# A transformer layer on 8 cores: the transposed `fc` weights are kept in DRAM, loads are merged, and two weight loads move ahead of their fences

## What is computed

```python
def _L0_attn_ref(x, W_q, W_kv, W_o):                 # H = 16 heads of 128
    q  = (x @ W_q.T).reshape(B, S, H, hd)
    kv = (x @ W_kv.T).reshape(B, S, H, hd)
    qf, kvf = fft(q), fft(kv)                        # over the head's 128
    qf, kvf = qf / |qf|, kvf / |kvf|                 # norm over the last axis
    kvf = cumsum(kvf, axis=1)                        # over the tokens
    values = ifft(qf * kvf).real.reshape(B, S, D)
    return values @ W_o.T

def _L0_ffn_ref(x, W_fc, W_proj):                    # 2048 -> 8192 -> 2048
    h  = square(relu(x @ ternary(W_fc).T))
    hn = h * rsqrt(mean(h * h) + eps)
    return hn @ ternary(W_proj).T

x = x + layernorm(_L0_attn_ref(layernorm(x), W_q, W_kv, W_o))
x = x + layernorm(_L0_ffn_ref(layernorm(x), W_fc, W_proj))
```

## Time and profile before

| | |
|---|---|
| time, 2 runs | 5866.28 and 5962.6 us, median 5914.44 |
| the profiled execution | 5843.32 us; span 5841.6 us on the slowest core (core 1) |
| cores' spans | 5798.1 to 5841.6 us |
| granted TensorE clock, mean | 0.77 on every core |
| stage 4 (feed-forward) | 3469 to 5841 us, 2372 us |

### The profile page before, as it was taken

One profiled execution on the slowest core, in us unless ns is written; L12 is line 12 of the kernel. 1 busy time (PEld: TensorE's weight loads), 2 busy tenths in 40 slices (PEclk: granted clock), 3 DMA queues, 4 the chain that ended last, 5 costly groups with the idle time before them and its releaser, 6 DMA issues.

```text
span 5841.6 us, 42698 instructions; the slowest of 8 cores (5798.1 to 5841.6 us)
## 1 busy us (share of the span) xinstructions
PE 3024.2 (52%) x12580; PEld 1194.8 (20%) x12580; DVE 2177.9 (37%) x2629; ACT 956.5 (16%) x1081; POOL 239.0 (4%) x420
## 2 busy tenths in 40 slices
PE   0404041404024024141455549994999589958995
PEld 0101010101001001010111114441334233423342
DVE  5465656561795791524122222103210221022202
ACT  2232323230232230101000011101110111001100
POOL 0000000000010010101000000000000000000000
PEclk9756565757557557575777789997999799979997
DMA  6353534354343435464742227544854375438542
GB/s 177 97 147 105 144 108 150 102 138 92 115 144 100 117 132 131 124 135 123 164 90 58 58 62 132 107 143 114 133 106 143 115 130 108 144 112 139 104 144 99
DMA packets 895779, 699.47 MB, mean 120 GB/s; under 512 B 694466, under 2 KB 768578, under 8 KB 879170
## 3 DMA queue, kind: packets, MB, share of 16 engines
q1 hardware_dynamic: 746178, 386.17, 28.7%
q0 software_dynamic: 68096, 201.35, 11.4%
q10 hardware_dynamic: 81280, 109.21, 7.7%
HBM read 411.24 MB, written 159.51 MB: 98 GB/s over the span
## 4 chain that ended last, share of the span: by engine, by line
PE 46%; DMA 20%; DVE 16%; issue 9%; another core or an unknown queue 4%; ACT 3%; SPq 2%; ACTq 0%; DVEq 0%; POOLq 0%; POOL 0%
PE pall L817 16%; PE pall L863 15%; PE pall L365 5%; DMA arena<-pj_t 5%; PE pall L710 4%; DVE arena L459 4%; DVE arena L441 4%; DMA pjT_t<-arena 3%; DMA arena<-b_scr 2%; SPq L802 2%; DMA fc_t<-arena 2%; DMA arena<-rq_scr 2%; DMA arena<-qn_scr 1%; PE pall L793 1%
## 5 line engine op out<-in xcount | busy, mean ns | idle before, releaser
L817 PE MATMUL pall<-arena 128*128 128x512 bf16 x4096 | 935.8, 382 | 43.9 <-DMA arena<-fc_t 32.8
L863 PE MATMUL pall<-arena 128*128 128x512 bf16 x4096 | 900.8, 383 | 30.7 <-DVE arena L871 27.0
L365 PE MATMUL pall<-arena 128*128 128x512 bf16 x2048 | 486.6, 393 | 651.8 <-DMA arena<-x_scr 216.0
L280 PE MATMUL pall<-arena,tones 128*1 128x512 bf16 x192 | 88.4, 469 | 853.7 <-DMA arena<-xT 632.4
L863 PEld LDWEIGHTS pall<-arena 128*128 128x128 bf16 x4096 | 403.8, 99 | 526.9 <-issue 54.4
L817 PEld LDWEIGHTS pall<-arena 128*128 128x128 bf16 x4096 | 382.5, 98 | 533.0 <-issue 112.9
L435 ACT ACTIVATE arena<-arena 128x2048 bf16<-128x2048 f32 x128 | 244.3, 1908 | 874.5 <-DMA pj_t<-arena 424.6
L827 DVE TENSOR_TENSOR arena<-arena 128x512 bf16<-128x512 bf16 x256 | 108.9, 425 | 743.5 <-ACT arena L824 743.5
L871 DVE TENSOR_TENSOR arena<-pall,rows 128x512 bf16<-128x512 f32 x64 | 44.3, 692 | 909.8 <-PE pall L863 903.7
L365 PEld LDWEIGHTS pall<-arena 128*128 128x128 bf16 x2048 | 195.8, 100 | 915.6 <-issue 716.7
L617 PE MATMUL pall<-arena,tdft 128*128 128x512 bf16 x64 | 37.6, 587 | 587.0 <-DMA arena<-qn_scr 587.0
(11 more groups left out here) (93 smaller groups left out, 2165.4 us busy)
## 6 DMA issues: line engine op xcount, KB each, us to landing
arena<-wfc SPq DMA_DIRECT2D x64, 1024.0 KB, 5.5
arena<-wproj SPq DMA_DIRECT2D x64, 1024.0 KB, 5.8
arena<-pjT_t SPq DMA_DIRECT2D x256, 256.0 KB, 2.7
arena<-pjT_t ACTq DMA_DIRECT2D x256, 256.0 KB, 2.7
fc_t<-arena POOLq DMA_DIRECT2D x64, 512.0 KB, 3.4
pj_t<-arena POOLq DMA_DIRECT2D x64, 512.0 KB, 4.5
pjT_t<-arena POOLq DMA_DIRECT2D x64, 512.0 KB, 3.0
arena<-xT POOLq DMA_DIRECT2D x8, 2048.0 KB, 15.7
```

The source lines that it names most:

```text
L365: last = h.matmul(pbks[i % 2], w3[:, k, m * P:(m + 1) * P], c2(src, k), start=(k == 0), stop=(k == NK - 1))
L817: last = h.matmul(bk(bi), pieces[pi][:, k * 1024 + m8 * P:k * 1024 + (m8 + 1) * P], c2(x3_bf, k), start=(k == 0), stop=(k == NK - 1))
L863: last = h.matmul(bk(j8), stripe[si][:, j8 * P:(j8 + 1) * P], c2(h2, m), start=(m == 0), stop=(m == NMH - 1))
```

## The change

1. 64 background steps are added between those of `pj_t` and `pjT`: `fcT_thunk(k, q4)` transposes a [2048, 128] piece of `fc_t` through `pt_buf` into the new DRAM tensor `fcT_t` [2048, 8192]. There are 256 steps now for the 298 places.
2. Stage 4's first pass loads an eighth with one plain DMA of 4 MB (128 x 16 rows of 2 KB) from `fcT_t`: on SP for the even eighths, on ACT for the odd ones.
3. The second pass loads two stripes with one DMA of 512 KB, into one of two buffers, in turn on SP and ACT.
4. The loads of `wkvT` and `woT` are recorded ahead of the fence instead of behind it. They go to the same SBUF space and wait for the last reader of the weights before.

```diff
+            def fcT_thunk(k, q4):
+                def thunk():
+                    em.dma("sync", lambda h: h.dma_start(
+                        out=pt_buf[0][:, :],
+                        in_=fc_t[q4 * D:(q4 + 1) * D, k * P:(k + 1) * P],
+                        transpose=True),
+                        reads=tuple(f"fct_{t}" for t in range(NMH)),
+                        writes=("ptb",))
+                    em.dma("gpsimd", lambda h: h.dma_start(
+                        out=fcT_t[k * P:(k + 1) * P, q4 * D:(q4 + 1) * D],
+                        in_=pt_buf[0][:, :]),
+                        reads=("ptb",), writes=(f"fcTt{k}",))
+                return thunk
+
+            for k in range(NK):
+                for q4 in range(HID // D):
+                    pwork.append(fcT_thunk(k, q4))
...
+        for kq in range(4 if PHASES >= 3 else 0):
+            em.dma("gpsimd", lambda h, kq=kq: h.dma_start(
+                out=wq_sb.rearrange("p (k m) -> p k m", m=D)[:, 4 * kq:4 * kq + 4, :],
+                in_=wkvT.rearrange("(k p) m -> p k m", p=P)[:, 4 * kq:4 * kq + 4, :]),
+                reads=(f"wq{kq}",), writes=(f"wq{kq}", f"wkv{kq}"))
+
         em.fence()
...
-        stripe = [ar.bf16(1024) for _ in range(4)]
+        stripe = [ar.bf16(2048) for _ in range(2)]
...
             for oct_ in range(8):
                 pi = oct_ % 2
-                for k in range(NK):
-                    em.dma("sync" if (k % 2 == 0 or not OPT & 4) else "scalar",
-                           lambda h, pi=pi, k=k, oct_=oct_: h.dma_start(
-                        out=pieces[pi][:, k * 1024:(k + 1) * 1024],
-                        in_=fc_t[oct_ * 1024:(oct_ + 1) * 1024,
-                                 k * P:(k + 1) * P], transpose=True),
-                        reads=FCT, writes=(f"pc{pi}_{k}",))
-                pks = tuple(f"pc{pi}_{k}" for k in range(NK))
+                em.dma("sync" if oct_ % 2 == 0 else "scalar",
+                       lambda h, pi=pi, oct_=oct_: h.dma_start(
+                    out=pieces[pi][:, :].rearrange("p (k e) -> p k e", e=1024),
+                    in_=fcT_t.rearrange("(k p) e -> p k e", p=P)
+                    [:, :, oct_ * 1024:(oct_ + 1) * 1024]),
+                    reads=FCTT, writes=(f"pc{pi}_0",))
+                pks = (f"pc{pi}_0",)
...
-                for m in range(NMH):
-                    si = m % 4
-                    em.dma("sync" if (m % 2 == 0 or not OPT & 2) else "scalar",
-                           lambda h, si=si, m=m, jo=jo: h.dma_start(
-                        out=stripe[si][:, :],
-                        in_=pjT_t[m * P:(m + 1) * P,
-                                  jo * 1024:(jo + 1) * 1024]),
-                        reads=PJT, writes=(f"st{si}",))
...
+                for mp in range(NMH // 2):
+                    sp = mp % 2
+                    em.dma("sync" if mp % 2 == 0 else "scalar",
+                           lambda h, sp=sp, mp=mp, jo=jo: h.dma_start(
+                        out=stripe[sp][:, :].rearrange(
+                            "p (mm e) -> p mm e", e=1024),
+                        in_=pjT_t.rearrange("(mm p) e -> p mm e", p=P)
+                        [:, 2 * mp:2 * mp + 2,
+                         jo * 1024:(jo + 1) * 1024]),
+                        reads=PJT, writes=(f"st{sp}",))
```

More of the change, by code:

```diff
@@ L197, in build_nc @@
     pjT_t = nc.dram_tensor("pjT_t", [HID, D], BF16, kind=_ikind).ap()
+    fcT_t = nc.dram_tensor("fcT_t", [D, HID], BF16, kind="Internal").ap()
     x1_scr = nc.dram_tensor("x1_scr", [D, SEQ], BF16, kind=_ikind).ap()
@@ L569, in build_nc @@
         B_t = [ar.bf16(T) for _ in range(2)]
-        for kq in range(4 if PHASES >= 3 else 0):
-            em.dma("gpsimd", lambda h, kq=kq: h.dma_start(
-                out=wkv_sb.rearrange("p (k m) -> p k m", m=D)[:, 4 * kq:4 * kq + 4, :],
-                in_=wkvT.rearrange("(k p) m -> p k m", p=P)[:, 4 * kq:4 * kq + 4, :]),
-                writes=(f"wkv{kq}",))
         WKVK = tuple(f"wkv{i}" for i in range(4))
@@ L661, in build_nc @@
             drain(8)
+        for kq in range(4 if PHASES >= 4 else 0):
+            em.dma("gpsimd", lambda h, kq=kq: h.dma_start(
+                out=wkv_sb.rearrange("p (k m) -> p k m", m=D)[:, 4 * kq:4 * kq + 4, :],
+                in_=woT.rearrange("(k p) m -> p k m", p=P)[:, 4 * kq:4 * kq + 4, :]),
+                reads=(f"wkv{kq}",), writes=(f"wkv{kq}", f"wo{kq}"))
         em.fence()
@@ L673, in build_nc @@
         bc23 = ar.bf16(2 * T)
-        for kq in range(4 if PHASES >= 4 else 0):
-            em.dma("gpsimd", lambda h, kq=kq: h.dma_start(
-                out=wo_sb.rearrange("p (k m) -> p k m", m=D)[:, 4 * kq:4 * kq + 4, :],
-                in_=woT.rearrange("(k p) m -> p k m", p=P)[:, 4 * kq:4 * kq + 4, :]),
-                writes=(f"wo{kq}",))
         WOK = tuple(f"wo{i}" for i in range(4))
@@ L772, in build_nc @@
         r_rms = rows[0:1, 3 * T + T // 2:3 * T + T].bitcast(BF16)
-        FCT = tuple(f"fct_{t}" for t in range(NMH))
+        FCTT = tuple(f"fcTt{t}" for t in range(NK))
         PJT = tuple(f"pjTt{m}" for m in range(NMH))
```

23 lines of the change are left out of this document (14 added, 9 removed).

## The result

The changed kernel takes 6734.38 us, the median of 11 runs; the kernel before, on the same chips, takes 5984.08, the median of 10. The ratio of their comparable runs is 1.141, with an interval from 1.132 to 1.150. The forecast was 6600, so the time came out 134 us above it: inside the range of 6410 to 6800, and above the 6520 to 6690 that the forecast had for itself. In a part of the executions of every kernel the cores of one die, or of both, show a lower granted clock and are some per cent slower; they are in the medians, whose difference of 750 us is therefore no measure of the change, and not in the ratios, and where an experiment met mostly such executions, its lowest run, or the cores without it, are compared. What the change adds is seen in the two profiled executions: 6667.64 - 5843.32 = 824 us, and 14.1% of the lowest 5866 is 825 too. The sum had +729, so it was 95 us short.

What follows compares the result with a forecast made beforehand. It took TensorE to bound stage 4 (feed-forward), with the transposing loads hidden. The sum 5843.3 - 4 + 230 + 0 - 10 + 448 + 35 + 30 = 6572, plus 28, gave 6600 us, range 6410 to 6800.

Steps and rivals of the forecast that it cites:

- Stripes as pairs: Stage 4's second pass: 512 KB loads land in 3.8 us against 3.52 of work, 0.12 us over 256 pairs, +30 us.
- The waits of the removed transposes: Stage 4: the transposing loads of fc_t are already hidden; 1 us a block comes back, -4 us, at most -44.
- 64 steps in stage 3: Stage 3 gets 78 background steps instead of 14, at 8.45 us each on POOL, with x_bf3 behind them: +230 us.
- Weight loads: wkvT and woT ahead of the fence: wkvT starts some 5 us earlier but x1g comes later, 0 us, within 15.
- Order at stage 2's third group: Stage 2: fcT's first transpose needn't wait for the last pj_t store, so one relay step goes, -10 us.
- The stalls: Stage 4's first pass: TensorE waits for odd eighths issued late by ACT, three 31 us and one 19 per block, +448 us.
- The clock after a stall: Stage 4's first pass: TensorE restarts at granted clock 0.50, losing 2.2 us behind each of 16 stalls, +35 us.
- The offset of 28: Whole kernel: 28 us added to the sum because two timed runs were 23 and 119 us above the profiled execution.
- Its own 4 MB only: Rival, stage 4's first pass: a stall waits only for ACT's load, 17 us, total about 6430 us; chance 0.15.
- Slower memory: Rival, stage 4: loads run at only 224 GB/s, lengthening stalls and pair landings, total about 6810 us; chance 0.13.
- Steps hidden: Rival, stage 3: the added steps are mostly hidden, +100 us instead of +230, total 6470 us; chance 0.07.
- Totals of the DMA engines only: Rival: only the DMA engines' total busy time counts, 36 us more hidden work changes nothing, some 5870 us; chance 0.03.

Runs made afterwards that it cites:

- all repairs: The changed kernel with all eighths loaded from SP, four pair buffers and two transpose buffers: 5907.10 us against 5907.31 for the kernel before, ratio 1.003.
- the second buffer: The kernel before with two transpose buffers (pt_buf) in turn instead of one: ratio 0.988, lowest run 5812.82 us beside 5847.10.

## Where the prediction held, and which of its steps failed

The sign, the mechanisms and the two heaviest terms held; the sizes did not. The time lies outside the forecast's own 6520 to 6690, and the sum's +729 us was +824. The step that failed by the largest factor is *Stripes as pairs*, the rule "with two buffers in turn half of the excess falls on each pair": +30 in the sum, +112 and +116 measured. Beside it the steps in stage 3 were 27 us too small, the slowest core's lower clock (80 us) had no term at all, and the stalls, at too low a rate, were 95 us too large, which hid the rest. Core by core, with core 4 against itself where nothing else is said:

- *The waits of the removed transposes, -4.* The idle time of the first pass that is not a wait for `fcT_t` is 40.7 us, where it was 43.9: 3 us came back. The 44 at the far end stay because the normalisation (L340) ends them, as the earlier trace rows had it.
- *64 steps in stage 3, +230.* Measured +257: 966 us in place of 709 (mean of the eight cores +262). Predicted was a step of 8.45 us, from a stretch of the first group. On core 7 the 78 stores take 718.6 us, with two stops; taking off 2 x 13 for these, (718.6 - 26)/77 = 9.0 us a step. Part of the steps come at 8 us and part at 9 to 10 or more, behind `x_bf3`'s load and at the relay's start. The bound that I gave for 8.9 was +265. The places of L767 were forecast at 3005, 3270 and 3523 and measured at 2989.51, 3271.71 and 3536.64: the first is early since the relay started 19 us sooner than I had it, and the drift behind it is the longer step. Stage 4's start near 3700 came at 3716.
- *Weight loads, 0.* From the issue of `wkvT` to the first projection it is 59.8 us in both kernels, by the mean of the cores. The experiment with this edit alone shows nothing either.
- *Order at stage 2's third group, -10.* Not seen. Core 7 issues this `x1g` at 2192.20, and did at 2193.02 before; from the second group's to the third's it is 422 us where it was 426, by the mean of the eight. The 2205.63 in the earlier trace rows is core 1's. `woT` is issued 8 us sooner than before on core 4, and by the mean of the eight cores 4 us later.
- *The stalls, +448.* Measured 353 to 361, in the predicted form of three long and one short per block and with the predicted cause: the wait fell to nothing when SP issued the loads. What was wrong in this term is the rate. I took 300 GB/s, from 2 MB of `x_scr` at 286 and the stripes. Two eighths, 8.39 MB, landed in 24.2 us, with the fixed 1.8 taken off 375 GB/s, and one in 14.0, which is 344. The long stall is then some 25 us and not 31, the short one 14 and not 19. That they share a path, on which 31 against 17 rested, holds: 15 us alone, 24 together. The Trainium skill, DMA: Bandwidth & Descriptors, section "Issuing engines are not separate DMA queues", says that DMAs of all issuers run on the same 16 engines and interleave. By that rule, the trace agrees, a load beside another takes longer than alone.
- *The clock after a stall, +35.* Measured +32 (968.9 - 936.6), which is 2.0 us for each of 16 stalls; the one in the rows above has 6.40 - 3.63 = 2.8.
- *Pairs, +30.* Measured +112 (idle 113.8 - 30.8, busy 928.1 - 898.9), and +116 with this edit alone. The excess was 3.8 - 3.52 by the forecast, with 3.6 of it for the landing. The load of 512 KB landed in 3.8. The waits at both ends of it stand on the path too, 0.11 us ahead and 0.14 behind; the matmuls of a pair that has waited take 3.63 and not 3.52; and a load that lands late, as the one of 4.25, is paid in full, one that lands early is not. 3.63 + 3.8 + 0.25 = 7.68 us for two pairs is 0.64 over 7.04, where the forecast had 0.24, and the measured 112/128 = 0.88 leaves the rest to late loads. My warning for this case, over 20 us a block, was met: 112/4 = 28.
- *The offset of 28.* The median lies 67 us above the profiled execution, and for the kernel before, in these runs, 141. The runs spread over more than 200 us in either kernel, and an offset from two runs was worth little.

The errors went against each other, and that the sum fits core 4 is luck: stalls -95, slow starts -3, pairs +82, transposes +1, and +29 for all that lies ahead of stage 4 (249 in place of 220). That is 14 us, and 744 - 729 = 15 were measured. The slowest core has 80 more, of which the lower clock is the larger part (97 us of slower matmuls, 24 us less of waiting). With the offset, 39 us more than the 28, these are the 134 us above the forecast.

The rivals. Its own 4 MB only: no, since a long stall takes 25 us and falls to 15.6 only when the other load is held back. Slower memory: no, it was faster than assumed. Steps hidden: no, some 255 us by themselves. Totals of the DMA engines only: no, but that was the right question for the kernel with all repairs, and even there it comes to no gain.

Whether the relay's longer step beside stage 3's other loads is due to the transposes or to the stores is open; the second buffer shows both growing.

## What to carry to other kernels

A load is a prefetch only if its issue does not stand behind work that depends on the data it should run beside: on a compute engine's own queue, the last activation of this tile is already too late for the next one, and one word ("sync") took away 353 us of stalls and 33 of slow starts. Count buffers in time: what is refilled in one period must land, with its waits, within that period, and two buffers of twice the size are not four buffers. And background work can cost nothing on the engines it uses but much on whatever is queued behind it, so its places deserve as much care as its amount: the kernel's own 64 steps in other places gave 131 us, where the change with all its repairs gave nothing. A last one, on reading profiles: the cores of one execution reach the same instruction 40 us and more apart here, so a gain of 10 us can't be read by setting one core of one profile against another core of the next.

## What the runs showed of the hardware

**A granted clock of 0.81.** The stretch 5560 to 5690 of the changed kernel, dense matmuls in both, on core 7 and on core 4:

```profile
5560.00:5690.00 130.00, 128.55 (x489) 51.62 (x487) 0.00 (x0) 0.00 (x0) 0.00 (x0) 0.81 0.42 122
```

```profile
5560.00:5690.00 130.00, 113.16 (x496) 47.58 (x496) 5.54 (x8) 0.00 (x0) 0.00 (x0) 0.96 0.42 126
```

Core 7 has 0.81 of full speed, which is neither of the two levels 0.50 and 1.00, and its matmuls take 128.55/489 = 0.263 us; at full clock it is 54.82/249 = 0.220 (stretch 4275 to 4335). By the trace's records of the clock, cores 6 and 7 spend over 600 us of this execution so, and core 4 none of stage 4. In the profile with the weight loads alone cores 0 to 3 have it for over 1100 us each, though nothing of stage 4 is changed there, and in the profile of before no core has it. So it doesn't take the change to bring it, and the slowest core was slower than core 4 by 85 us, most of it so, though both run the same program. When it comes is open; in stage 4 of the changed kernel it was seen on neighbouring pairs of cores (0 and 1, 6 and 7).

**Rates.** All eight cores active, two loads of 4 MB with rows of 2 KB ran at 323 GB/s on core 7 over the whole stall and, by an estimate from the median landing of 24.2 us less the prediction's 1.8, at some 375 in flight, where 2 MB of `x_scr` had run at 286.

**A transpose and a store in each other's way.** With one buffer 4.5 and 3.0 us to landing, with two 6.4 and 4.9: a second buffer brought a step from 8.45 us to 5.8 to 6.3, and not to the 4 to 5 expected.
